# A three-stage transformer block on one core: score queries split by batch instead of by head group, the first tile's loads reordered, and the contexts' block transfers issued by ScalarE

## What is computed

```python
q = layernorm(x) @ Wq                       # [64, 16 heads, 32, 64]
k, v = ctx @ Wk, ctx @ Wv                   # [64, 16 heads, 257, 64]
probs = softmax(einsum('bhsd,bhkd->bhsk', q, k) / 8)
x = x + einsum('bhsk,bhkd->bhsd', probs, v) @ Wo + bo      # cross attention
x = x + self_attention(layernorm(x))        # 16 heads, relative position bias
x = x + quantized_ffn(layernorm(x))         # fake-quantized silu(gate) * up, down
```

## Time and profile before

| what | before |
|---|---|
| median of 3 runs | 1573.8 us (1572.8 to 1575.11) |
| the profiled execution's own time | 1573.21 us |
| its span | 1571.4 us |
| TensorE busy | 1511.5 us, 96% of the span |
| VectorE, ScalarE, GpSimd busy | 1121.0, 731.6, 385.6 us |
| mean granted TensorE clock | 0.989 |
| transfers | 235.90 MB, 150 GB/s over the span, all but 1.34 MB of it on queue q1 |

### The profile page before, as it was taken

One profiled execution on the slowest core, in us unless ns is written; L12 is line 12 of the kernel. 1 busy time (PEld: TensorE's weight loads), 2 busy tenths in 40 slices (PEclk: granted clock), 3 DMA queues, 4 the chain that ended last, 5 costly groups with the idle time before them and its releaser, 6 DMA issues.

```text
span 1571.4 us, 35367 instructions
## 1 busy us (share of the span) xinstructions
PE 1511.5 (96%) x13421; PEld 1259.9 (80%) x13421; DVE 1121.0 (71%) x2240; ACT 731.6 (47%) x1532; POOL 385.6 (25%) x225
## 2 busy tenths in 40 slices
PE   7999877999999999999999999999999999998989
PEld 6888777888888988889988898878878878786544
DVE  7666758877778777787778877656555564556788
ACT  5444635555455554555455554433223232224755
POOL 1000233444444454444544444400000000000000
PEclk9999979999999999999999999999999999999999
DMA  7899795446554555545654464250310311323022
GB/s 241 317 368 362 289 307 155 109 145 172 166 170 98 161 169 169 165 102 171 169 169 142 115 180 145 89 194 22 110 67 29 124 40 42 108 82 129 2 106 107
DMA packets 148590, 235.90 MB, mean 150 GB/s; under 512 B 75345, under 2 KB 101393, under 8 KB 145681
## 3 DMA queue, kind: packets, MB, share of 16 engines
q1 hardware_dynamic: 148496, 234.57, 46.5%
HBM read 165.59 MB, written 68.94 MB: 149 GB/s over the span
## 4 chain that ended last, share of the span: by engine, by line
PE 85%; issue 7%; DVE 4%; DMA 3%; ACT 1%; SPq 0%; POOLq 0%; POOL 0%; DVEq 0%; ACTq 0%
PE psum_o L670 16%; PE psum_q L647 8%; PE psum_s L647 8%; PE psum_o L1482 6%; PE psum_q L1522 6%; PE psum_q L698 6%; PE psum_q L1482 6%; PE psum_t L1554 6%; PE psum_o L562 5%; PE psum_o L685 5%; PE psum_t L658 3%; DMA c_blk<-in_ctx_dram 2%; PE psum_s L1509 1%; PE psum_t L594 1%; PE psum_q L594 1%
## 5 line engine op out<-in xcount | busy, mean ns | idle before, releaser
L670 PE MATMUL psum_o<-pT,c_nat 128*128 128x512 f32 x1152 | 283.9, 397 | 27.1 <-issue 14.7
L670 PEld LDWEIGHTS psum_o<-pT,c_nat 128*128 128x128 f32 x1152 | 212.8, 189 | 76.7 <-issue 16.6
L1272 POOL TENSOR_TENSOR c_nat<-c_raw,constants 128x768 fp32r<-128x768 f32 x64 | 109.1, 1704 | 500.1 <-PE psum_o L670 386.7
L861 ACT ACTIVATE probs<-psum_s,nmax 128x257 f32<-128x257 f32 x128 | 61.1, 477 | 297.9 <-DVE nmax L1150 297.9
L647 PE MATMUL psum_s<-cT_high,qk 128*128 128x258 f32 x768 | 167.6, 294 | 0.1
L647 PE MATMUL psum_q<-cT_high,qk 128*128 128x258 f32 x768 | 153.8, 286 | 2.5 <-DVE qk L1063 2.5
L1136 DVE TENSOR_SCALAR oT<-psum_o,c_last 128x512 f32<-128x512 f32 x192 | 139.2, 745 | 21.9 <-PE psum_o L670 21.9
L928 DVE TENSOR_TENSOR pT<-psum_t,pT 128x512 fp32r<-128x512 f32 x128 | 87.7, 686 | 77.3 <-ACT pT L742 77.3
L1257 POOL TENSOR_TENSOR c_raw<-c_raw,last_row 128x768 f32<-128x768 f32 x64 | 118.0, 1843 | 65.4 <-DMA last_row<-in_ctx_dram 50.0
L647 PEld LDWEIGHTS psum_s<-cT_high,qk 128*128 128x128 f32 x768 | 130.1, 193 | 3.9 <-DVE cT_low L1113 0.6
L647 PEld LDWEIGHTS psum_q<-cT_high,qk 128*128 128x128 f32 x768 | 124.2, 189 | 5.6 <-DVE qk L1063 2.9
(11 more groups left out here) (299 smaller groups left out, 3364.8 us busy)
## 6 DMA issues: line engine op xcount, KB each, us to landing
qk_by_tile<-staged SPq DMA_DIRECT2D x32, 1536.0 KB, 10.4
raw<-qk_by_tile SPq DMA_DIRECT2D x16, 3072.0 KB, 13.9
c_raw<-in_ctx_dram SPq DMA_DIRECT2D x64, 384.0 KB, 3.5
c_blk<-in_ctx_dram SPq DMA_DIRECT2D x256, 96.0 KB, 2.4
last_row<-in_ctx_dram SPq DMA_DIRECT2D x64, 192.0 KB, 5.1
x_res<-in_x_dram SPq DMA_DIRECT2D x16, 256.0 KB, 2.6
out_dram<-x_res SPq DMA_DIRECT2D x16, 256.0 KB, 2.0
x_in<-out_dram SPq DMA_DIRECT2D x4, 1024.0 KB, 7.3
```

What stands on the lines that cost most here:

```text
L670: i = pe.matmul(ps[:], c_nat[(b - 1) % 2][:, part, k, m * P:(m + 1) * P], pT[:, moving, k, :], start=(k, part, moving) == (0, 0, 0), stop= ...
L1272: G.tensor_tensor(flat(c_nat[i][:, 0, :, :]), flat(c_raw[i][:]), zero.to_broadcast([P, 2 * DC]), ALU.add).then_inc(s_chi, 1)
```

## The change

Five edits, which belong together:

1. The split of `qk` goes by batch: `qk_of(part, b)` and `raw_of(b)` cut slice `b` of all heads. TensorE waits for low part `b` at the first score block of batch `b`, instead of for one `rg` at each block of batch 0. Four slices of 128x1536 remain four slices of 128x1536.
2. The work on the slices moves. In the loop, slices 0 and 1 of the next tile are made at the end of batch 3 (ScalarE after the last exponential, VectorE after `dve_attended` 1), slices 2 and 3 in the tile itself: ScalarE at the end of batch 0, VectorE in batch 1 after the turn. "first" and "second" have places of their own. GpSimd makes the low parts of slices 0 and 1 of tile 0, as it did for `rg` 0 and 1.
3. `load_blocks` is called by ScalarE after its last exponential of each batch (in the projection after the high part of context 0, in tile 0 after that of context 1), and so runs on ScalarE's queue.
4. SP's list loses the blocks and the waits for `s_nat` ahead of `load_ctx` (but one). `raw` of the next tile is issued in batch 1, after the wait for its four low parts; in "second" in batch 0. In "last" the loads of `x_in2` and `w2q_raw` move from batch 0 to batch 1 with it. At the seam the wait for the stores comes after `raw` of tile 1, and `wv`, `bo`, `x_res` go ahead of context 4 and `wo_raw`.
5. In the projection's last group, the turn, high part and low part of context 0 move from the QK steps into the Q steps 4 to 6; in tile 0, the transposes of batch 1 come after its second score block.

The diff, cut to its core:

```diff
...
                 pe.wait_ge(s_ctlo, 4 * t + (b + 1))
-            if b == 0:
-                pe.wait_ge(s_qlo, 4 * t + (rg + 1))
+                pe.wait_ge(s_qlo, 4 * t + (b + 1))
             ps, done = empty(pe, U1(("S", b, rg), t, section))
...
                 before = begun or b > 0
+                late = not begun and b == 1
                 pe_scores(pe, t, b, 0, section)
-                if before:
+                if before and not late:
                     pe_probsT(pe, t, b, section)
                 pe_scores(pe, t, b, 1, section)
+                if late:
+                    pe_probsT(pe, t, b, section)
                 pe_scores(pe, t, b, 2, section)
...
-        def act_qk_high(act, t, rg):
+        def raw_of(b):
+            return raw[:].rearrange("p h r (c b q) -> p b (r c) h q", c=KC, b=4)[:, b]
+        def qk_of(part, b):
+            return qk[:, part].rearrange("p r c b (h q) -> p b (r c) h q", h=4)[:, b]
+        def act_qk_high(act, t, b):
...
             act.wait_ge(s_qraw, 16 * t + 16)
-            nc.scalar.activation(qk[:, 0, rg, :, :, :].rearrange("p c b (h q) -> p h (c b) q", h=4),
-                                 raw[:, :, rg, :].rearrange("p h (a q) -> p h a q", q=SQ), ACT.Copy).then_inc(s_qhi, 1)
+            nc.scalar.activation(qk_of(0, b), raw_of(b), ACT.Copy).then_inc(s_qhi, 1)
...
                     act_group_q(act, s, j)
+                    if (s, j) == (GROUPS - 1, 4):
+                        act_last_column(act, 0, 0)
+                    if (s, j) == (GROUPS - 1, 5):
+                        act_context_high(act, 0, 0)
+                        load_blocks(act, 0, 1)
                 if s < GROUPS - 1:
                     act_group_x(act, s + 1)
-                else:
-                    act_last_column(act, 0, 0)
-                    act_context_high(act, 0, 0)
                 for j in range(4, 8):
                     act_group_qk(act, s, j)
-                    if s == GROUPS - 1 and j in (4, 5):
-                        act_qk_high(act, 0, j - 4)
-            for rg in range(2, 4):
-                act_qk_high(act, 0, rg)
+                    if s == GROUPS - 1 and j in (4, 6):
+                        act_qk_high(act, 0, j // 2 - 2)
...
                 act_last_column(act, 4 * t, 1)
+                act_context_high(act, 4 * t, 1)
+                load_blocks(act, 4 * t, 2)
                 exp(0, 0)
                 exp(0, 1)
-                act_context_high(act, 4 * t, 1)
                 scale(0, 0)
...
                 exp(0, 3)
+                act_qk_high(act, t, 2)
                 act_last_scalars(act, t, 0, section)
...
                     act_probsT(act, t, b, k, section)
-                if b == 3 and more:
-                    act_qk_high(act, t + 1, 0)
                 exp(b, 1)
...
                 scale(b, 1)
+                if (section, b) == ("first", 1):
+                    act_qk_high(act, t, 3)
+                if (section, b) == ("first", 3):
+                    act_qk_high(act, t + 1, 0)
+                if (section, b) == ("second", 0):
+                    act_qk_high(act, t, 2)
                 if b == 1 and section == "second":
...
                 exp(b, 3)
+                if more or b < 2:
+                    load_blocks(act, 4 * t, b + 2)
                 if b == 3 and more:
+                    if begun:
+                        act_qk_high(act, t + 1, 0)
                     act_qk_high(act, t + 1, 1)
                 act_last_scalars(act, t, b, section)
+                if b == 0:
+                    if section != "second":
+                        act_qk_high(act, t, 2)
+                    act_qk_high(act, t, 3)
                 if b == 3 and not more:
                     act_weight(act, "q")
-                if b == 3 and more:
-                    act_qk_high(act, t + 1, 2)
-                    act_qk_high(act, t + 1, 3)
...
-        def dve_qk_low(dve, t, rg, section=None):
-            if section:
-                full(dve, U1(("S", 3, rg), t - 1, section))
-            dve.wait_ge(s_qhi, 4 * t + (rg + 1))
-            part = [qk[:, i, rg, :, :, :].rearrange("p c b (h q) -> p h (c b) q", h=4) for i in range(2)]
-            nc.vector.tensor_tensor(part[1], raw[:, :, rg, :].rearrange("p h (a q) -> p h a q", q=SQ), part[0].bitcast(F32),
-                                    ALU.subtract).then_inc(s_qlo, 1)
+        def dve_qk_low(dve, t, b):
+            dve.wait_ge(s_qhi, 4 * t + (b + 1))
+            nc.vector.tensor_tensor(qk_of(1, b), raw_of(b), qk_of(0, b).bitcast(F32), ALU.subtract).then_inc(s_qlo, 1)
...
                     dve_turn(dve, 4 * t, b + 1)
+                if (section, b) == ("first", 1):
+                    dve_qk_low(dve, t, 3)
+                if (section, b) == ("first", 3):
+                    dve_qk_low(dve, t + 1, 0)
+                if (section, b) == ("second", 0):
+                    dve_qk_low(dve, t, 2)
+                if b == 1 and section not in ("first", "second"):
+                    dve_qk_low(dve, t, 2)
+                    dve_qk_low(dve, t, 3)
                 if b == 1 and section == "second":
...
                     inverse(b, 2)
-                if qk_next:
-                    dve_qk_low(dve, t + 1, 0, section)
                 dve_attended(dve, t, b, 0, section)
                 inverse(b, 3)
-                if qk_next and not begun:
-                    dve_context_low(dve, 4 * t, b + 1)
-                    dve_qk_low(dve, t + 1, 1, section)
-                    norm(b, 2)
-                    norm(b, 3)
-                    dve_attended(dve, t, b, 1, section)
-                    dve_qk_low(dve, t + 1, 2, section)
-                    dve_qk_low(dve, t + 1, 3, section)
-                    dve_attended(dve, t, b, 2, section)
-                    continue
-                if qk_next:
-                    dve_qk_low(dve, t + 1, 1, section)
                 if after:
...
                 dve_attended(dve, t, b, 1, section)
-                if qk_next:
-                    dve_qk_low(dve, t + 1, 2, section)
-                    dve_qk_low(dve, t + 1, 3, section)
+                if b == 3 and more:
+                    if begun:
+                        dve_qk_low(dve, t + 1, 0)
+                    dve_qk_low(dve, t + 1, 1)
+                if (section, b) == ("second", 0):
+                    dve_qk_low(dve, t, 3)
                 if not more and b == 3:
...
-        def load_blocks(sp, batch, ahead):
+        def load_blocks(eng, batch, ahead):
...
             if not isinstance(batch, int) or batch + ahead:
-                sp.wait_ge(s_turn, batch + ahead)
+                eng.wait_ge(s_turn, batch + ahead)
             keys = ctx_of(batch, ahead)
...
                 quarter = keys[:, 0:2 * P, f * QUARTER:(f + 1) * QUARTER]
-                sp.dma_start(c_blk[KEYS * f:KEYS * (f + 1), :, :],
+                eng.dma_start(c_blk[KEYS * f:KEYS * (f + 1), :, :],
                              quarter.rearrange("a (k n) d -> n (a k) d", n=KEYS)).then_inc(s_blk, 16)
...
                                  staged[:, j % 4, :, :, :].rearrange("p t r n -> p t (r n)")).then_inc(s_staged[j % 4], 16)
-                    if (s, j) == (GROUPS - 1, 4):
-                        load_blocks(sp, 0, 1)
+                    if (s, j) == (GROUPS - 1, 3):
                         sp.wait_ge(s_nat, 1)
...
                         load_x_group(sp, s + 2)
+            load_ctx(sp, 0, 3)
+            sp.wait_ge(s_qlo, 4)
+            load_qk(sp, 0, 1)
             for i in range(4):
                 sp.wait_ge(s_staged[i], 32 * GROUPS)
-            load_blocks(sp, 0, 2)
-            sp.wait_ge(s_nat, 2)
-            load_ctx(sp, 0, 3)
-            load_qk(sp, 0, 1)
-            load_blocks(sp, 0, 3)
-            sp.wait_ge(s_nat, 3)
-            load_ctx(sp, 0, 4)
-            sp.dma_start(wo_raw[:], Wo.rearrange("(k p) n -> p k n", p=P)).then_inc(s_wo, 16)
             sp.dma_start(wv[:], Wv.rearrange("(k p) n -> p k n", p=P)).then_inc(s_wvo, 16)
...
             sp.dma_start(x_res[:], rows(x_rows, 0)).then_inc(s_xres, 16)
-            load_blocks(sp, 0, 4)
-            sp.wait_ge(s_nat, 4)
+            load_ctx(sp, 0, 4)
+            sp.dma_start(wo_raw[:], Wo.rearrange("(k p) n -> p k n", p=P)).then_inc(s_wo, 16)
             load_ctx(sp, 0, 5)
-            load_blocks(sp, 0, 5)
...
                 if more or b < 2:
-                    load_blocks(sp, 4 * t, b + 2)
-                    sp.wait_ge(s_nat, 4 * t + (b + 1))
                     load_ctx(sp, 4 * t, b + 2)
-                if b == 0:
+                if b == (0 if section == "second" else 1):
                     sp.wait_ge(s_qlo, 4 * t + 4)
...
```

More of the change, by code:

```diff
@@ L1088, in dve_project_all @@
                     dve_group_q(dve, s, j)
+                    if (s, j) == (GROUPS - 1, 4):
+                        dve_turn(dve, 0, 0)
+                    if (s, j) == (GROUPS - 1, 6):
+                        dve_context_low(dve, 0, 0)
```

(35 more changed lines are left out.)

## The result

The changed kernel takes 1586.4 us (median of 4 runs, 1582.7 to 1588.0) against 1573.3 (4 runs, 1572.1 to 1575.1): 1.0079 times as long, 95% interval 1.0058 to 1.0100. The prediction said 1550, so it was wrong, in sign too. The profiled execution is one of 1588.0 us with a span of 1586.0, 14.6 above that of before.

A forecast was written before the change was run, and what follows sets the result against it. TensorE, busy for 96% of the span, bounds the kernel, so only its idle time can give. Terms -17 - 2 - 6.5 + 2 = -23.5 gave 1549.7, with the median's 0.6 1550 us; range about 1531 to 1568.

The forecast's parts named there:

- Blocks in the loop: Loop, blocks 3 issued by ScalarE with raw under way: landing at 378.1 for a turn at 377.9, counted as nothing.
- rival D: Batch 3's turn, each loop tile: blocks 3 land at 382.4, TensorE loses 3.9 us a tile, 1601 us; chance 0.08.
- Rival B: Loop: queues alternate by packets, blocks 3 finish with raw, about 379.4; TensorE loses 0.9 us a tile, 1562 us; chance 0.20.
- Seam and tile 0: Start of tile 0 to tile 1: earlier start and fewer waits gain 17 us, bounds 8 and 26.
- Rival C: Tile 0: transfer engines already full, waits only change name, gain only the lower bound of 8, 1559 us; chance 0.09.
- Tile 1: Tile 1: four low parts no longer precede it in a row; gain 2 us, bounds 3.8 and a loss of 1.
- The loop's two other terms: Loop, tile's end and batches 0 and 1: 1.2 us gained, 0.7 given back, net 0.5 a tile, 6.5 for 13.
- the gain of 1.2 us a tile at the tile's end: Loop, first pe_pv of a tile: two low parts leave, so 0.82 us idle and 0.37 of slow restart go.
- The 0.7 that batches 0 and 1 were to give back: Loop: 4.7 us of ScalarE work in a 3.2 us gap; TensorE waits and restarts slowly, losing 0.7 of 1.2 us.
- rival A: Loop: ScalarE's issues are nearly free, so it gives 15.6 us instead of 6.5, 1541 us; chance 0.20.
- The wait of 0.5 us that I had worked out: Loop, batch 1: TensorE wants bank o1 for pe_pv at 368.2, VectorE's low part frees it at 368.7.
- Last tile: Last tile: x_in2 moved to batch 1 lands 1 to 2 us too late for VectorE; loss 2 us, bounds 0 and 5.

The follow-up runs named there:

- e2: The changed kernel, blocks still on ScalarE's queue, but in each loop tile SyncE issues raw only once blocks 3 have landed: 1561.7 us.
- e1: The changed kernel with the blocks' loads back in SyncE's list, ahead of load_ctx of the same batch: 1545.1 us, 0.9832 of before.
- e6: The changed kernel, blocks on ScalarE's queue, every large load held back until blocks landed, contexts 4 and 5 ahead of wv and wo_raw: 1546.7 us.
- e8: e1 with slices of qk in tiles 0 and 1 moved behind the next heads' low part, ScalarE's high parts with them: 1550.1 us.
- e9: e1 with the loop's four qk slices again made at the tile's end and raw loaded in batch 0, as before the change: 1559.0 us.

## Why the prediction was wrong

*Blocks in the loop* is the step that failed: "I count nothing". Measured: 1.8 us a tile (the change against e2), 24 us in all, which by itself eats the forecast's gain of 23.5. Tile 0 and tile 1 came out 16 and 7 us above their terms, the rest of the loop 8 us better than its own, and the last stretch 0.7; together that is about the 38 us between the forecast's sum (1549.7) and the profiled run (1588.0).

The step misread first. Their 7.8 us is the median from a transfer's own issue to its landing, and I added it to the first of four issues. The fourth was issued at 366.5 and took the longest, 8.7 us, so the blocks were complete at 375.2, 10.3 us after the first issue. From 370.3 that is 380.6, 2.7 us behind the turn at 377.9 and past rival D's 380.3: the rows that the forecast leaned on already had the loss in them. The change took the same 10.2 us. What shrank is the time until VectorE is ready to turn, from 13.4 us (364.90 to 378.28) to 8.1 (375.80 to 383.9). Before, SyncE issued blocks 3 right behind the turn that frees `c_blk`; ScalarE issues them 5.2 us behind it (its end is at 370.6), and `raw`, moved from 359.0 to batch 1, has been issued just ahead of them. I called it "under way" and did not ask how fast blocks pass beside it.

In two queues the transfer engines alternate by packets (49 to 49), and 384 bytes against 24 KB is no share. One list keeps order, and that helps only a load that stands ahead: in the kernel before, 42 of the 128 packets of `raw` had passed (those of over 8 KB from 359.0 to 364.9) when blocks 3 were issued behind it, and they too waited for the rest (from 364 to 369 no packet under 8 KB passed). With `raw` through at about 383 and 1024 packets at 468 to 525 a us, blocks behind it in one list would also have been there near 385 or 386. This is an estimate; no run has that order in the loop. So the runs show the cost of blocks beside a `raw` begun before them, not that two queues are worse than one list in that order.

Rival B named this mechanism; its size was wrong. It had the blocks land with `raw`, at 379.4 in its clock, and 0.9 us a tile. They land 1.3 us behind it (386.0 against 384.7), since hardly any has passed when its last packets go: loss 1.8. That is rival D's threshold, "a loss of 1.8 us a tile", though D's own price was 3.9; that the kernel is slower, and not merely no faster, took tiles 0 and 1 as well. Together they had 0.28, too little for the one part of which no row existed. The rule in DMA: Bandwidth & Descriptors, section Queues, rings and completion order, of the Trainium skill, cited with B, agrees with the counts of 49 to 49, 535 to 537 and 52 to 47.

*Seam and tile 0*: forecast -17, bounds 8 and 26. Measured -0.6, outside the bounds. The worst case let a block take 12.8 us; it took 18.0, beside three large loads. Rival C expected that the waits would only change name because the transfer engines are full; but their share is 0.95 in tile 0 of e1 and 0.74 in the change, so they were less busy in the slow kernel, and tile 0 of e1 is 44.7 us. With the starvation away (e1, e6) tile 1 starts at 230.6 and 231.2, 14 us earlier than before: the term was 3 too high even so. TensorE's waits behind a slice of `qk` between the maxima are 2.3 to 2.7 us, and not half of 1.7; that they make up the 3 us is not shown, since e8 took them away and other waits came.

*Tile 1*: forecast -2, measured +4.7. TensorE is busy 51.5 us instead of 49.7, at a mean granted clock of 0.96 of 2.4 GHz instead of 1.00. Starved blocks are not the cause of that: e1 has 51.6 us at 0.95. e1 has tile 1 at +2.0, with a wait of 2.6 us behind the slice in batch 0; e6, which adds ScalarE's issues, is 2.5 above e1. I had costed none of these.

*The loop's two other terms*: the gain of 1.2 us a tile at the tile's end was right (e1 1.25, e9 1.18). The 0.7 that batches 0 and 1 were to give back was not: e6 gives back 0.08 against e1. Four issues do take ScalarE 1.9 us (375.80 to 377.7), as on SyncE, so rival A's premise is false, but its loop, 15.6 us shorter or 48.55 a tile, is the one measured once nothing large runs beside the blocks (e6, 48.58). In the change itself, the low part that frees bank o1 began at 373.96 and ended at 374.6, and TensorE went on to `pe_pv` at 374.77 without a pause. The wait of 0.5 us that I had worked out never came.

*Last tile*: forecast +2, measured +2.0, by another cause: VectorE waits 2.19 us for blocks beside `w2q_raw` and `x_in2`, TensorE 1.80. e1 has +0.5.

For the change with its blocks in SyncE's list (e1) the forecast's 1550 stands against 1545. Part of that nearness is luck: tiles 0 and 1 came out 7 us worse than their terms and the loop 10 us better.

## What to carry to other kernels

A second DMA queue is not a fast lane: in these runs a load of many small packets beside one of few large packets in another queue got one packet for each large one, whichever engine began it, and landed when the other was through. Behind the large one in the same list it was no faster (10.3 us before). Put urgent small loads ahead of large ones in one list, or hold the large one until they have landed; then it does not matter which engine issues them. Before a load is moved, look at what is issued within its own landing time on every queue, count packets, not bytes, and measure from the first issue to the last landing.

## Not expected of the hardware

Blocks on a second queue passed 16 packets a us beside packets of 24 KB, 178 beside packets of 1.5 KB, and 468 with nothing beside them. `raw` itself is hardly slowed by them (10.5 us to land in the tile read, 10.6 in e1's), but cut into pieces of 1.5 KB it moves 0.27 MB a us beside blocks, against 0.40 in pieces of 24 KB. Whether blocks of fewer, larger packets would hold their own was not tried: their layout in `c_blk` sets 384 bytes.
